# Graph aggregation, recurrence and routed experts on one core: where the row norm, the W2 centring and two small columns are computed

## The reference

```python
# block 1: graph aggregation and a recurrence, 128 steps
beta  = layernorm(x) @ e_weight / max(sum(adj, 2), 1e-7)
agg   = einsum('blu,blm->bmu', beta, adj)
h     = tanh(agg[:, t] @ Wx + h @ Wh + b)       # for t in 0..127
x     = x + all h
# block 2: routed experts on every one of the 16384 rows
z     = layernorm(x)
logit = z @ gate_w + gate_b                     # 16 experts
top2  = top_k(logit, 2);  w = softmax(top2 values)
y     = z + sum over both of w * (relu(z @ w1[e] + b1[e]) @ w2[e] + b2[e])
x     = x + layernorm(y) * gamma + beta
```

## Time and profile before

| | us |
|---|---|
| median of 3 runs | 715.17 (713.19 to 716.28) |
| profiled execution, its own time | 712.58 |
| span of its trace | 710.7 |
| aggregation | 0 to 74 |
| first tanh of the recurrent stage | 74.6 |
| first and last scatter of the recurrent stage start | 93.7 and 285.9 |
| second part | from 291.2 (first row load issued) |

### The profile page before, as it was taken

The page is one execution under the profiler, slowest core; times in us unless marked ns, Lnnn a source line. Parts: engine busy times, 40 slices in busy tenths (PEclk is TensorE's granted clock), DMA queues, the critical chain, the costliest instruction groups (busy, mean ns, idle before and its releaser), DMA issues.

```text
span 710.7 us, 17699 instructions
## 1 busy us (share of the span) xinstructions
PE 545.0 (77%) x4140; PEld 486.8 (68%) x4140; DVE 523.0 (74%) x2695; ACT 376.8 (53%) x1185; POOL 500.3 (70%) x557
## 2 busy tenths in 40 slices
PE   2666897988888872399999999900799999999920
PEld 1555575765666661299999999900799999999920
DVE  5996697887877775188888888700299899999850
ACT  2999443333333320266666666500588888888810
POOL 3677568888888887167777777776067777777774
PEclk9999999898988955599999999955699999999975
DMA  8999469322323213369876665441997676664110
GB/s 244 273 283 304 127 217 258 103 81 89 92 88 94 73 49 114 76 191 324 282 244 207 198 198 179 154 152 28 302 318 223 192 219 203 197 210 143 46 51 7
DMA packets 115094, 121.37 MB, mean 171 GB/s; under 512 B 19017, under 2 KB 99613, under 8 KB 115008
## 3 DMA queue, kind: packets, MB, share of 16 engines
q1 hardware_dynamic: 95936, 76.79, 37.7%
q0 software_dynamic: 17920, 43.03, 16.7%
q10 hardware_dynamic: 1152, 0.56, 0.3%
HBM read 68.67 MB, written 55.90 MB: 175 GB/s over the span
## 4 chain that ended last, share of the span: by engine, by line
PE 38%; ACT 7%; POOL 7%; issue 4%; DMA 1%; DVE 1%; SPq 0%; POOLq 0%; ACTq 0%; DVEq 0%
PE bank L931 19%; PE bank L947 15%; ACT hs L999 5%; POOL rows_by_second L212 4%; POOL out_dram L212 3%; PE bank L920 3%; ACT xT L980 2%; PE bank L944 2%; DMA R<-rows_by_second 0%; DMA rows_by_second<-R 0%; DMA R<-rows_by_first 0%; ACT wr L988 0%; SPq L856 0%; ACT L1008 0%; SPq L858 0%
## 5 line engine op out<-in xcount | busy, mean ns | idle before, releaser
L212 POOL DMA_INDIRECT out_dram<-R x144 | 143.2, 995 | 67.5 <-issue 39.0
L212 POOL DMA_INDIRECT rows_by_second<-R x144 | 144.7, 1005 | 62.3 <-issue 35.1
L947 PE MATMUL bank<-W,hs 128*128 x1152 | 176.8, 290 | 0.0
L999 ACT ACTIVATE hs<-bank,wr 128x128 f32<-128x128 f32 x432 | 127.1, 366 | 87.6 <-PE bank L931 81.8
L931 PE MATMUL bank<-xT,wr 128*128 128x128 f32 x1152 | 158.9, 282 | 7.1 <-ACT xT L980 7.1
L947 PEld LDWEIGHTS bank<-W,hs 128*128 128x128 f32 x1152 | 152.4, 193 | 3.8 <-issue 0.2
L931 PEld LDWEIGHTS bank<-xT,wr 128*128 128x128 f32 x1152 | 143.1, 196 | 14.4 <-ACT xT L980 14.4
L212 POOL DMA_INDIRECT rows_by_first<-st x128 | 126.7, 989 | 35.7 <-issue 33.8
L1068 DVE SCALAR_TENSOR_TENSOR R<-bank,R 128x128 f32<-128x128 f32 x288 | 87.3, 344 | 66.2 <-PE bank L947 62.7
L988 ACT COPY wr<-W1b 128x258 f32 x288 | 104.9, 426 | 17.1 <-PEq L802 17.0
L537 ACT ACTIVATE HT<-bank,bcol 128x128 f32<-128x128 f32 x128 | 46.7, 364 | 95.2 <-PE bank L450 93.9
(11 more groups left out here) (132 smaller groups left out, 856.9 us busy)
## 6 DMA issues: line engine op xcount, KB each, us to landing
R<-rows_by_second SPq DMA_DIRECT2D x144, 196.0 KB
R<-rows_by_first SPq DMA_DIRECT2D x144, 68.0 KB
xq<-in_x_dram SPq DMA_DIRECT2D x32, 256.0 KB, 3.6
aq<-in_adj_dram SPq DMA_DIRECT2D x32, 256.0 KB, 4.2
x2r<-in_x_dram SPq DMA_DIRECT2D x32, 256.0 KB, 2.8
rows_by_second<-filler SPq DMA_DIRECT2D x1, 3136.0 KB, 13.2
rows_by_second<-filler SPq DMA_DIRECT2D x16, 196.0 KB
rows_by_second<-R POOLq DMA_INDIRECT x144
```

The source lines that it names most:

```text
L212: return nc.gpsimd.indirect_dma_start(dst, bass.IndirectOffsetOnAxis(ap=idx, axis=0), src, None, bounds_check=limit[n], oob_is_err=False)
L947: i = mm(o, hs[:, h, c, k * P:(k + 1) * P], W2[:, bass.ds(e[k], 1), c, :].rearrange("p o f -> p (o f)"), start=False, stop=c == 1, skip_gr ...
L999: i = a(hs[:, h, c, k * P:(k + 1) * P], ps_h[c][h][:, k * P:(k + 1) * P], ACT.Relu, bias=wr[:, u % 2, 2 * h + k, F + c:F + c + 1])
```

## The change

The reciprocal root leaves GpSimd. VectorE computes it by an integer first guess and two steps of third order, nine instructions of 128x4 elements: `root_0` (guess), then twice `square`, `against`, `inner`, `outer`. Each waits for the one before it through a new semaphore `s_root`; the last one writes the root and raises `s_r2`. They belong to quad q-1 and stand between the gate's parts of quad q-2.

Six instructions leave VectorE's turn. The three of the W2 centring become two on ScalarE (`w2_mean` with an accumulator, in step 2; `w2_centre` in step 3). The token column is copied on ScalarE (`tokens`, step 0), the softmax sum 1 + exp as well (`sums`, right after `exps`). `C_NMR` and its instruction are gone: the statistics are written straight into the row, which now keeps the mean, and `zed` computes (x - mean) * rstd. `send` on GpSimd waits for `s_tok` and `s_w1` besides `s_d`. ScalarE's loop now holds eight quads instead of four.

```diff
-C_RSTD, C_NMR, C_W1, C_W2, C_TOKEN, C_POS1, C_POS2, C_SPARE = range(P, P + 8)
+C_MEAN, C_RSTD, C_W1, C_W2, C_TOKEN, C_POS1, C_POS2, C_SPARE = range(P, P + 8)
...
-            def rstd(q, u):
-                h = u % 2
-                pool.wait_ge(s_v2, q + 1)
-                g.tensor_tensor(st[:, u, :, C_RSTD], ve2[:, h, :], mhalf[:, 0:QUAD], ALU.pow).then_inc(s_r2, 1)
-
             def send(q, u):
 
+                hold(pool, s_tok, q + 1)
+                pool.wait_ge(s_w1, q + 1)
                 hold(pool, s_d, q + 1)
...
+            def sums(q, u):
+                act.wait_ge(s_ex, q + 1)
+                a(den[:, u % 2, :], ex[:, u % 2, :], ACT.Identity, bias=unit[:, :]).then_inc(s_den, 1)
+
+            def tokens(q, u):
...
+                if beyond(q, SLOTS):
+                    act.wait_ge(s_sct[u % SLOTS], 64 * (q - u % SLOTS) // SLOTS)
+                nc.scalar.copy(st[:, u % SLOTS, :, C_TOKEN].bitcast(I32),
+                               tok[:, bass.ds(QUAD * q, QUAD)]).then_inc(s_tok, 1)
...
+            def w2_mean(q):
...
+                a(w2junk[:, :], w2v[:, bass.ds(q, 1), :].rearrange("p o f -> p (o f)"), ACT.Identity, scale=-1.0 / P,
+                  accum_out=w2m[:, bass.ds(q, 1)]).then_inc(w2_ok, 1)
+
+            def w2_centre(q):
+                hold(act, w2_ok, 2 * q + 1)
+                w = w2v[:, bass.ds(q, 1), :].rearrange("p o f -> p (o f)")
+                a(w, w, ACT.Identity, bias=w2m[:, bass.ds(q, 1)]).then_inc(w2_ok, 1)
...
-            quads(act, steps)
+            quads(act, steps, SLOTS)
...
+            def root_0(q, u):
+
+                dve.wait_ge(s_v2, q + 1)
+                v.tensor_scalar(root_y[:, u % 2, :].bitcast(I32), ve2[:, u % 2, :].bitcast(I32), -0.5, ROOT_BITS,
+                                ALU.mult, ALU.add).then_inc(s_root, 1)
+
+            def square(n):
+                def part(q, u):
+                    h = u % 2
+                    dve.wait_ge(s_root, 8 * q + 4 * n + 1)
+                    v.tensor_tensor(root_a[:, h, :], root_y[:, h, :], root_y[:, h, :], ALU.mult).then_inc(s_root, 1)
+                return part
...
-                order = ((tile_a, 1), (soft_1, 3), (tile_b, 1), (soft_2, 3), (place_1, 3), (tile_b2, 1), (place_2, 3),
-                         (soft_3, 3), (tile_b3, 1), (gate_1, 2), (place_3, 3), (gate_2, 2), (gate_3, 2),
-                         (centre_1, 0), (gate_4, 2), (centre_2, 0), (gate_5, 2), (centre_3, 0))
+                order = ((tile_a, 1), (soft_2, 3), (tile_b, 1), (soft_3, 3), (place_1, 3), (tile_b2, 1), (place_2, 3),
+                         (tile_b3, 1), (gate_1, 2), (root_0, 1), (place_3, 3), (sq_0, 1), (gate_2, 2),
+                         (ag_0, 1), (gate_3, 2), (in_0, 1), (gate_4, 2), (ou_0, 1), (sq_1, 1), (gate_5, 2), (ag_1, 1),
+                         (in_1, 1), (ou_1, 1))
...
                         i = v.tensor_scalar(R[:, u, j, C_Z:C_Y], R[:, u, j, 0:P],
-                                            R[:, u, j, C_RSTD:C_RSTD + 1], R[:, u, j, C_NMR:C_NMR + 1],
-                                            ALU.mult, ALU.add)
+                                            R[:, u, j, C_MEAN:C_MEAN + 1], R[:, u, j, C_RSTD:C_RSTD + 1],
+                                            ALU.subtract, ALU.mult)
```

More of the change, by code:

```diff
@@ L92, in build @@
         b2m = sb("b2m", [P, 1])
[L93 removed]
+        w2m = sb("w2m", [P, 2 * NE])
+        w2junk = sb("w2junk", [P, P])
         sel = sb("sel", [P, NE, P], BF16)
@@ L165, in build @@
         s_sct = [sem(f"s_sct{i}") for i in range(SLOTS)]
-        s_dd, s_ex, s_w1, s_hot, s_nm, s_cnt, s_pos, s_sel, s_red, s_d, s_den, s_chain = (
-            sem("s_" + k) for k in ("dd", "ex", "w1", "hot", "nm", "cnt", "pos", "sel", "red", "d", "den", "chain"))
+        s_dd, s_ex, s_w1, s_hot, s_tok, s_cnt, s_pos, s_sel, s_red, s_d, s_den, s_chain = (
+            sem("s_" + k) for k in ("dd", "ex", "w1", "hot", "tok", "cnt", "pos", "sel", "red", "d", "den", "chain"))
         padded, starts, tables = sem("padded"), sem("starts"), sem("tables")
@@ L550, in _ @@
             exps(NQ - 2, UN - 2)
+            sums(NQ - 2, UN - 2)
             exps(NQ - 1, UN - 1)
+            sums(NQ - 1, UN - 1)
             act.wait_ge(starts, 1)
@@ L604, in tile_b3, with against, part, inner @@
                     dve.wait_ge(s_r2, q - 1)
-                v.tensor_scalar(ve2[:, u % 2, :], mvs[:, u % 2, :, 1], LN_EPS, None, ALU.add).then_inc(s_v2, 1)
+                v.tensor_scalar(ve2[:, u % 2, :], st[:, u, :, C_RSTD], LN_EPS, None, ALU.add).then_inc(s_v2, 1)
+            def root_0(q, u):
[8 more added lines that the diff above has]
+                return part
+            def against(n):
+                def part(q, u):
+                    h = u % 2
+                    dve.wait_ge(s_root, 8 * q + 4 * n + 2)
+                    v.tensor_tensor(root_b[:, h, :], root_a[:, h, :], ve2[:, h, :], ALU.mult).then_inc(s_root, 1)
+                return part
+            def inner(n, scale):
+                def part(q, u):
+                    h = u % 2
+                    dve.wait_ge(s_root, 8 * q + 4 * n + 3)
+                    v.scalar_tensor_tensor(out=root_a[:, h, :], in0=root_b[:, h, :], scalar=-10 / 3 * scale ** 2,
+                                           in1=root_b[:, h, :], op0=ALU.add, op1=ALU.mult).then_inc(s_root, 1)
+                return part
+            def outer(n, scale):
+                def part(q, u):
+                    h = u % 2
+                    dve.wait_ge(s_root, 8 * q + 4 * n + 4)
+                    y = root_y[:, h, :]
+                    i = v.scalar_tensor_tensor(out=st[:, u, :, C_RSTD] if n else y, in0=root_a[:, h, :],
+                                               scalar=5 * scale ** 4, in1=y, op0=ALU.add, op1=ALU.mult)
+                    i.then_inc(s_r2 if n else s_root, 1)
+                return part
+            sq_0, ag_0, in_0, ou_0 = square(0), against(0), inner(0, ROOT_0), outer(0, ROOT_0)
+            sq_1, ag_1, in_1, ou_1 = square(1), against(1), inner(1, ROOT_1), outer(1, ROOT_1)
             def gate_1(q, u):
```

62 lines of the change are left out of this document (30 added, 32 removed).

## The result

| | before | after |
|---|---|---|
| median, us (7 runs each) | 715.05 (712.77 to 716.28) | 710.89 (709.59 to 712.16) |
| profiled execution | 712.58 | 710.99 |
| span | 710.7 | 709.0 |

The ratio is 0.994 [0.9921, 0.9959]. The change makes the kernel 0.6% faster, 4.2 us. The forecast was 698.6 and its range ended at 709: the sign was right, three quarters of the gain did not come.

The account below looks back on a forecast made before the run. GpSimd was taken as the bound at 6.12 us a quad, then VectorE at 5.35. Up to quad 8 +0.3, 23 turns -10.1, tail -6.8: -16.6 us, giving 696.0 profiled, 698.6 by the median; range 690 to 709.

Parts of the forecast that it names:

- VectorE's turn: VectorE's instructions per quad: 4.94 us now, -0.07 up to the index search, +0.48 behind it, giving 5.35.
- ScalarE's additions: Four instructions a quad on ScalarE, expected to be hidden; uncovered, all four would cost 1.2 us a quad.
- rival D: ScalarE's longer loop stalls where it branches back, two times 3.0 us uncovered: 704.6 us; chance 0.09.
- rival E: ScalarE's additions land in the tanh chain and a quad takes 6.6 us: slower, 727 us; chance 0.04.
- Branch stalls: VectorE's two waits where its loop branches back, 3.01 and 2.91 us, expected to stay and enter the path.
- The tail: From the last `tile_a` to the last scatter: 24.0 us before, 17.2 expected after, -6.8.
- part two: Program behind the last scatter: starts on that scatter and does the same work, 0 change.
- pitch of 0.07: VectorE's small instructions with independent work between them were taken to follow each other at 0.07 us.
- link of 0.20: A VectorE root instruction that needs the previous one's result was taken to start 0.20 us after it.
- The load for quad 8: x2r load ahead of quad 8's `tile_a`: taken to land no earlier than 122.9; `tile_a` at 123.2, +0.3 us.
- The first row: Recurrent stage from the first tanh to `tile_a` of quad 0: predicted difference 0.
- rival C: TensorE or VectorE's waits cost more: ten of 23 quads at 6.0 us, or turns of 5.7; 706 us; chance 0.16.

Follow-up runs that it names:

- power back, moves stay: Changed kernel with the power back on GpSimd and no root instructions on VectorE; centring, token column and softmax sum stay on ScalarE: 715.23 us, ratio 0.9998.
- root alone: Kernel before with only the root moved to VectorE; centring, token column, C_NMR and softmax sum stay on VectorE: 719.55 us, ratio 1.006.
- changed, written out: Changed kernel with all 32 turns of VectorE written out, no loop: 697.72 us, ratio 0.9745.
- changed, root spread: Changed kernel with the second root step's last three instructions moved into the next turn behind other work, and `hot` ahead of `sq_1`: 696.18 us, ratio 0.9724.
- all three: Changed kernel with weight loads behind the last x2r load, VectorE's turns written out and the last three root instructions one turn later: 689.16 us, ratio 0.9627.
- written-out kernel before: Kernel before with all 32 turns of VectorE written out, no loop: 714.67 us, ratio 0.9996.

## Why the prediction was wrong

| kernel | VectorE's own turn | GpSimd's quad | median |
|---|---|---|---|
| before | 4.94 | 6.12 | 715.05 |
| power back, moves stay | 4.64 | 6.12 | 715.23 |
| root alone | 5.99 | waits | 719.55 |
| changed | 5.66 | waits | 710.89 |
| changed, written out | 5.38 | waits | 697.72 |
| changed, root spread | 5.07 | waits | 696.18 |
| all three | under 5.12 | 5.12 | 689.16 |

(Before, with the power back: one turn less its wait for GpSimd. Root alone and below: means as above.)

**Held.** GpSimd was saturated (the power back and the written-out kernel before both give 715). The scatters need 5.12 a quad. The bound moves to VectorE. ScalarE's additions are hidden, and rival D's loop stall and rival E did not come: in the changed trace the tanh at which quad 16 begins follows 0.94 behind the one before, an ordinary step. Branch stalls enter the path. The tail shrinks, part two is neutral.

**The step that failed is VectorE's turn: 5.66, not 5.35.** Piece by piece, the prediction had 2.41, 0.83, 1.10 and 1.01, and the changed kernel without its loop has 2.35, 0.90, 1.10 and 1.03 = 5.38. So the pitch of 0.07 and the link of 0.20 were right for straight-line code, and the item that was left out is the loop: 0.28 of the 0.31. The prediction took its pitches from one turn of the kernel before, whose loop costs 0.07 a turn, and put the price of the new body at nothing. In one term this can be named: from `ou_1` to `tile_a` it had 0.07, and it is 0.20 in the loop, 0.11 written out. That undoing the loop takes 0.28 a turn off is shown. The obvious suspect is the register arithmetic that a loop needs ahead of waits on a value that depends on the step (67 such instructions in eight turns, 43 before). It may explain the 0.09 ahead of `tile_a`. It does not explain the holes: all eight turns have it at the root's links, where it costs nothing, and the holes stand elsewhere, each in its own turn. Their cause is open. Price: 23 x 0.31 = 7.1.

**The load for quad 8 was taken as a fixed time.** "The load lands no earlier" than 122.9 and the bound of 124.2 rested on it. It lands when VectorE's quad 3 lets it. The seven turns from quad 0 to 7 took 36.37 us, before 32.98, and a full wait for the load came on top of them. Of the 3.21 from quad 0 to quad 8, 1.9 come from the later quad 3 and 1.3 from the weight loads between, which took that much longer. Price: 3.21 - 0.3 = 2.9.

**Smaller ones.** Branch stalls 6.54 instead of 5.92, 0.6. The tail 18.44 instead of 17.2, 1.2: GpSimd stalls 1.68 before the scatter at 265.71, the second of quad 28 and so in the last quad of its loop; the twelve scatters behind it start at 269.55 and not at 268.2. All seven kernels with both root steps on VectorE have this stall (1.39 to 1.68). The one with a single step doesn't have it, nor do those where GpSimd still computes between its scatters. The cause is not shown. The first row gives 1.04 back, by the way of counting alone.

Together -16.6 + 7.1 + 2.9 + 0.6 + 1.2 - 1.0 = -5.8, where the profile shows -5.54. Without the first row it is -4.8, where the profile shows -4.50 and the medians -4.2.

**The choice.** The bounds of the turn were 5.0 and 5.8, and the true 5.66 lay inside; rival C had "or if a turn costs 5.7: 706" at 0.16. That number came true, C's mechanism did not: C named TensorE's round and VectorE's waits for it, and the changed trace has no wait of VectorE for TensorE in a plain turn; it is TensorE that waits for `hot`, as it did before. The range missed because the load's 2.9, the 0.6 of the branch stalls and the 1.2 of the tail were not added to that end. The Trainium skill ("Runtime: NRT & Kernel Launch", "Instruction fetch mechanics") calls runtime control flow expensive and prefers full unrolling; the 13.2 us of the written-out kernel agree, and the 0.3 us of the same edit on the kernel before, no clear difference, show that it holds only where nothing covers the engine.

## What to carry to other kernels

Before work is taken from a saturated engine, cost the next engine's whole turn as it will then stand in the path: its dependent links, what its loop adds to branch stalls and to each turn, and every load whose buffer it frees; all of these look free as long as someone else is the bound. Put the links of a chain of small operations far apart in the order, over the turn's seam if need be: here that alone was worth more than three times what the change gave. And a load that lands late has a chain behind it; follow it back to the buffer it waited for before taking its time as given.

## What the hardware showed that was not expected

- The loop form of the same turn takes 0.28 us more (5.66 against 5.38), with no releaser in the trace, mostly as holes that come back at the same place every eight turns.
- `root_0`, a multiply and add on 128x4 int32, took 0.15, 0.16, 0.41 and 0.29 us in four turns in a row, and again every eight turns. It is the place in the loop and not the instruction: written out, 30 of 32 take 0.15 to 0.17.
- An activation with an accumulator issues a second instruction. ScalarE, `w2_mean`:

```profile
199.42 0.30 ACT L575 ACTIVATE w2junk<-W 128x128 f32 x1
199.62 0.19 ACT L575 ACTIVATION_READ_ACCUMULATOR w2junk<-W  x1
```

- A scatter behind a real wait started about 0.8 us after its releaser's end (202.20 to 203.01), against the 0.30 between queued ones.
- Giving four links cover saved 0.59 a turn (5.66 to 5.07), where 4 x 0.13 = 0.5 was to be had by pitch and link; the rest was not traced.
